# Linear attention with routed experts on one core: the state sets in a row, results a quad later, scatters in batches

## The reference

```
xn = layernorm(x)                            # x: 8 x 1024 x 128, float32
q, k, v = xn @ W_qkv, 16 heads of 8; k = layernorm(k) within each head
S = 0; for each chunk of 64 tokens:
    y = S q + causal(q k^T) v;  S = S + v^T k
attn = y @ W_o
e    = argmax(xn @ centroids.T)              # one of 8 experts a token, 8192 tokens
xh   = layernorm(xn) * ln_g[e] + ln_b[e]
h    = relu(w1[e] @ xh + b1[e])              # 512 wide
ffn  = xn + sigmoid(xn . centroid[e]) * (w2[e] @ h + b2[e])
out  = x + attn + ffn
```

## Time and profile before

| what | value |
|---|---|
| device time, 3 runs | 392.41 us median, 391.08 to 395.75 |
| profiled execution: its span | 363.3 us |
| between that span and the median | 29.1 us |
| mean granted clock of TensorE | 0.986 |

### The profile page before, as it was taken

The page is one execution under the profiler, slowest core; times in us unless marked ns, Lnnn a source line. Parts: engine busy times, 40 slices in busy tenths (PEclk is TensorE's granted clock), DMA queues, the critical chain, the costliest instruction groups (busy, mean ns, idle before and its releaser), DMA issues.

```text
span 363.3 us, 17565 instructions
## 1 busy us (share of the span) xinstructions
PE 342.1 (94%) x6868; PEld 293.0 (81%) x6868; DVE 287.1 (79%) x799; ACT 241.8 (67%) x657; POOL 251.7 (69%) x245
## 2 busy tenths in 40 slices
PE   6799999998999999999999989999999999999991
PEld 6466786776787687777867879999999999999990
DVE  8888897898886888878877786788777788777860
ACT  4788687677587666757566735766666667666660
POOL 3488477789788765556455513888888888888884
PEclk9989999999999999999999999999999999999996
DMA  6220433636314021545553445555545555555420
GB/s 196 70 60 8 118 91 97 184 104 194 106 47 120 19 87 54 157 109 163 150 152 93 131 105 134 72 73 72 72 65 74 71 63 74 74 76 59 38 23 0
DMA packets 55153, 33.18 MB, mean 91 GB/s; under 512 B 5352, under 2 KB 52768, under 8 KB 55072
## 3 DMA queue, kind: packets, MB, share of 16 engines
q1 hardware_dynamic: 42800, 23.53, 23.9%
q0 software_dynamic: 12272, 8.54, 17.2%
HBM read 18.72 MB, written 13.78 MB: 89 GB/s over the span
## 4 chain that ended last, share of the span: by engine, by line
issue 25%; POOL 13%; PE 11%; DVE 1%; DMA 1%; POOLq 1%; ACT 1%; SPq 0%; DVEq 0%; ACTq 0%
POOL out_dram L494 13%; PE bank L1328 2%; PE sc L1274 2%; PE bank L1337 2%; PE bank L1222 1%; DMA out_dram<-res 1%; POOLq L71 1%; PE bank L1200 1%; PE bank L1306 1%; DVE pr L856 1%; PE bank L1209 1%; PE bank L1295 1%; PE bank L1255 1%; PE bank L1215 0%; PE bank L1233 0%
## 5 line engine op out<-in xcount | busy, mean ns | idle before, releaser
L494 POOL DMA_INDIRECT out_dram<-qx,rows x71 | 112.9, 1590 | 35.1 <-issue 22.1
L694 ACT ACTIVATE qx<-sc,b1T 128x128 f32<-128x128 f32 x280 | 79.8, 368 | 39.6 <-PE sc L1421 39.6
L420 POOL DMA_INDIRECT slots_d<-rows,pos_i x64 | 64.2, 1003 | 43.1 <-issue 11.0
L856 DVE TENSOR_TENSOR pr<-sc,causal 128x1536 f32<-128x1536 f32 (+2 forms) x33 | 63.6, 1929 | 17.4 <-PE sc L1274 17.2
L1429 PE MATMUL bank<-tokens,qx 128*128 128x128 f32 x568 | 75.3, 276 | 0.8 <-ACT qx L694 0.7
L1421 PE MATMUL sc<-wide,tokens 128*128 128x128 f32 x560 | 74.0, 275 | 0.2 <-issue 0.2
L1429 PEld LDWEIGHTS bank<-tokens,qx 128*128 128x128 f32 x568 | 69.0, 192 | 1.4 <-ACT qx L694 1.4
L1421 PEld LDWEIGHTS sc<-wide,tokens 128*128 128x128 f32 x560 | 68.1, 192 | 0.3 <-issue 0.3
L1015 DVE COPY tokens<-xT 128x1024 f32 x71 | 55.2, 778 | 0.0
L1274 PEld LDWEIGHTS sc<-qx,kT 32*64 32x64 f32 x2048 | 32.5, 132 | 16.4 <-issue 15.8
L1030 DVE SCALAR_TENSOR_TENSOR qx<-bank,rows,qx 128x128 f32<-128x128 f32 x71 | 24.9, 350 | 26.3 <-PE bank L1429 25.8
(11 more groups left out here) (167 smaller groups left out, 532.2 us busy)
## 6 DMA issues: line engine op xcount, KB each, us to landing
rows<-slots_d SPq DMA_DIRECT2D x71, 66.0 KB, 2.0
res<-in_L_attn_x_dram SPq DMA_DIRECT2D x16, 256.0 KB, 4.1
out_dram<-res SPq DMA_DIRECT2D x16, 256.0 KB, 3.4
tokens<-in_L_attn_x_dram SPq DMA_DIRECT2D x7, 512.0 KB, 4.2
w1raw<-in_L_ffn_w_dram SPq DMA_DIRECT2D x8, 256.0 KB, 4.0
w2raw<-in_L_ffn_w_dram SPq DMA_DIRECT2D x8, 256.0 KB, 4.3
out_dram<-qx,rows POOLq DMA_INDIRECT x71, 3.4
slots_d<-rows,pos_i POOLq DMA_INDIRECT x64
```

Source lines behind the costliest of these rows:

```text
L420: pool.indirect_dma_start(slots_d, bass.IndirectOffsetOnAxis(ap=pos_i[:, t:t + 1], axis=0), rows[:, t, :], None, bounds_check=E * RT * P - ...
L494: pool.indirect_dma_start(out_rows, bass.IndirectOffsetOnAxis(ap=xs[:, a, D + 2:D + 3].bitcast(U32), axis=0), ye[:, a, :], None, bounds_ch ...
L694: last = nc.scalar.activation(ht[:, k % 2, c * P:(c + 1) * P], inner(k)[:, c * P:(c + 1) * P], ACT.Relu, bias=b1T[:, bass.ds(e * FC + c, 1)])
L856: nc.vector.tensor_tensor(pr[:, h % 2, a:G, w].rearrange("p g (j t) -> p g j t", t=CH), sc[:, a * BANK:G * BANK].rearrange("p (g w) -> p g ...
```

## The change

Four parts, in all engines' orders. (1) TensorE does `products(2n-1)`, then `state_step(n)`, `inter_second(n-1)` and `inter_first(n)` behind each other; the middle state's share is added a quad later, so `y_copy` and the output of quad n - 1 wait for it. The first state difference moves from the Y bank to FB (quad 0 apart), the affinities' back transposes and the ranks to FB and into the next quad's first half, and the second transpose of a quad's end from FB to a Y bank. (2) At a quad's end the order of ScalarE is: transposes, `values_across`, `ln_root` for the quad after; VectorE has `ln_inverse` and `ln_shift` ahead of the first mask. (3) ln_g and ln_b are applied in `se_xT` as scale and bias, w1 is copied unscaled, and the fold, `b1T`, `lbb` and its load go. (4) GpSimd sends three rows behind the quad's first mask in quads 3 to 8 (two more in 7 and 8), and from quad 9 four and three a quad.

```diff
@@ tensor: the quad loop
-                scores(h)
-                if h % 2 == 0:
-                    if more:
-                        kT_project(n + 1)
-                    state_step(n)
-                    if h:
-                        products(h - 1)
-                    inter_first(n)
-                    if more:
-                        k_transpose(n + 1)
-                    if n and out_early(n):
-                        output(n - 1)
-                    if more:
-                        q_project(n + 1)
-                else:
-                    products(h - 1)
...
+                scores(2 * n)
+                if n:
+                    products(2 * n - 1)
+                    state_step(n)
+                    inter_second(n - 1)
+                    inter_first(n)
+                if n in (2, 4, 6, 8):
+                    affinities_back(n // 2 - 1)
+                if n in (3, 5, 7, 9):
+                    rank_tokens(n // 2 - 1)
+                if more:
+                    kT_project(n + 1)
+                if n == 0:
+                    state_step(0)
+                if more:
+                    q_project(n + 1)
+                    k_transpose(n + 1)
+                if n and early:
+                    output(n - 1)
...
+                scores(2 * n + 1)
+                products(2 * n)
+                if n < 8 and n % 2 == 1:
+                    affinities(n // 2)
+                if more:
+                    v_project(n + 1, FB)
...
@@ tensor: kT_project
-                    second_left(n - 2)
+
+                    pe.wait_ge(s("dsta_sb"), n)
+                if n in (3, 5, 7, 9):
+                    pe.wait_ge(s("aff_sb"), n // 2)
+                if n in (4, 6, 8, 10):
+                    pe.wait_ge(s("rank_sb"), n // 2 - 1)
@@ gpsimd
+            for n in range(LATE):
+                norm = n + 1 < NCH
+                mask_scores(2 * n)
+                if n >= 3:
+                    send_rows(3 if norm else 3)
+                if norm:
+                    ln_norm(n + 2, range(4))
+                    ln_norm(n + 2, (4,))
+                mask_scores(2 * n + 1)
+                state_middle(n)
+                if not norm:
+                    send_rows(2)
+                state_end(n)
+                if n + 1 < LATE:
+                    values_own(n + 1)
@@ scalar: expert stage
-                nc.scalar.activation(xsT[:, k % 2, :], SC[k % 2][:, 0:P], ACT.Copy).then_inc(s("sex_sb"), 1)
...
+                of = SC[k % 2][:, 0:P] if k > 1 else FB[:, k * P:(k + 1) * P]
+                nc.scalar.activation(xsT[:, k % 2, :], of, ACT.Identity, scale=gT[:, bass.ds(e, 1)],
+                                     bias=lbT[:, bass.ds(e, 1)]).then_inc(s("sex_sb"), 1)
@@ vector
-            def b1_fold(e):
...
+                if norm:
+                    ln_inverse(n + 2)
+                    ln_shift(n + 2)
+                if n == 0:
+                    dstate_first(n)
+                score_mask(2 * n)
+                if n:
+                    dstate_first(n)
```

397 lines of the change are left out of this document (164 added, 233 removed).

## The result

The changed kernel takes 435.02 us (median of 4 runs, 433.27 to 436.62) against 391.75 us (4 runs, 389.93 to 395.75) for the kernel before: a ratio of 1.1085, 95% interval 1.1009 to 1.1161. The forecast was 393.4 with a range up to 399. It is wrong by 42 us.

The account below looks back on a forecast made before the run. TensorE's own instructions were taken to set the quads' pace except in 3 and 5. Terms +1.7 +3.2 +1.4 -1.2 -4.0 -0.1 = +1.0 took the span from 363.3 to 364.3; with 29.1 carried, 393.4 us, range 386.5 to 399.

Parts of the forecast that it names:

- The base of the sum: Whole kernel: the 29.1 us between the profiled span of 363.3 and the median of 392.4 was carried unchanged.
- Scatters in the late quads, seven of 1.28 in 11.7, fit: GpSimd in late quads: seven scatters of 1.28 us fit in a quad of 11.7, costed at nothing.
- Quads 10 to 14: Late quads: each takes 11.75 us instead of 12.54, 4.0 us gained in all, bounds nothing to 6.
- K + 7.6: Late quads: the next quad starts 7.6 us after the k projection's start K, at 11.7 from the quad's start.
- the waits hide the small stalls on issue: Late quads, TensorE: small issue stalls, one of 0.32 us, are hidden by waits, so a quad is taken at 11.75.
- The gain from fewer changes of tile shape: TensorE, each quad: 7 changes of tile shape instead of 11 at 0.15 us, up to 0.6 us of 12.5.
- Early even quads: Quads 2, 4 and 6: norm steps and state difference delay the k projection, 13.4 us each, +3.2 in all.
- Quads 3 and 0: Quad 3: GpSimd's three sends delay its normalised rows, 15.6 us, +1.4; quad 0: VectorE's norm steps go first, +1.7.
- Quads 1, 5, 7, 8, 9: These quads end 0.2, 0.25, 0.4, 0.0 and 0.4 us earlier, -1.2 in all, bounds -3 and +2.
- Fold, scale and bias: Fold leaving VectorE, scale and bias in ScalarE's expert-row copy: +0.07 us a slot, bounds 0 and 0.2, hidden, costed at nothing.
- The rivals: Three alternatives: TensorE bound everywhere, 383.4 or 388, chance 0.25; GpSimd bound, 398.1, 0.25; drains saved needlessly, 397.4, 0.05.
- GpSimd becomes the bound of quads 3 to 6: Rival: GpSimd's 13.1 us a quad grows to 14 or more, +5.7 in all, 398.1 us; chance 0.25.

Follow-up runs that it names:

- b1_before: The kernel before, unchanged, profiled a second time: 388.49 us, span 386.7.
- e1_spread: The changed kernel with its scatters one at a time again as before the change, each behind its own signal: 417.94 us, 1.0675 of before.
- e5_light: The changed kernel with scatters in threes, released behind the state sets and the first products, ahead of TensorE's long instructions: 419.44 us, 1.0717 of before.
- e2_batched: The kernel before with only its scatters batched as the change does it: 430.20 us, 1.1008 of before.
- e3_held: The changed kernel with all 64 scatters held back until behind the last quad: 475.39 us.
- e7_plain: The changed kernel with plain DMAs of the same bytes in the batches' places and the true scatters behind the last quad: 472.09 us.
- m2_late_norm: e3_held with VectorE's two norm steps moved back behind the mask and the first state difference: 466.07 us.
- e9_before_held: The kernel before with its 64 scatters held back behind the last quad: 448.75 us.
- n1_fold: The kernel before with only VectorE's fold and its load removed and scale and bias applied in ScalarE's copy: 389.26 us, 1.0008 of before.
- e6_landed: The changed kernel with single scatters as in e1_spread, each from quad 9 also waiting until the one before has landed: 470.62 us.

## Why the prediction was wrong, step by step

**The base of the sum.** "The page gives no time of its own beside the span, so I carry the 29.1 us between it and the median of 392.4 unchanged." This is the step that failed first. Around the span lie 1.8 us (b1_before: 388.49 less 386.7). The spans of b1_before and of the earlier trace rows are 23.4 us apart, time in which the scatters starved TensorE, in the timed executions and not in the profiled one; the other 3.9 are what the median of 392.4 is above b1_before's 388.5. A cost of the scatters was so carried over as a constant, though the change moves the scatters. All that I read from the earlier trace rows for quads 3 to 14 was of an execution that is not like those timed. It also hid the one resource that the change loads harder. 29.1 us is 7% of the time and should have been a question.

**"Scatters in the late quads, seven of 1.28 in 11.7, fit", at nothing.** They fit on GpSimd. They cost TensorE 236.7 - 208.2 = 28.5 us over the quads in the kernel before, single (b1_before), and 283.7 - 233.6 = 50.1 in the changed one, batched: +21.6. With the order's 25.4 (233.6 - 208.2) that makes 47.0, and the spans are 433.8 - 386.7 = 47.1 apart (the medians of the one round that timed both 43.3). By e1_spread's profile against that of the changed kernel, undoing the batches wins 14 of the 21.6 (269.5 against 283.7 at the last scores); but that execution is the slowest of its four, and by the medians it is 17. By e5_light a part of this may be the place and not the batching.

The two sums don't simply add, either. In the kernel before the batches cost more than in the changed one: e2_batched has its last scores at 278.3, so 278.3 - 208.2 = 70.1. On top of batches the new order costs 283.7 - 278.3 = 5.4 and without any scatter 25.4. So the scatters' new places alone bring nearly the whole loss, and so far as they are there, the order adds little.

**Quads 10 to 14, "5 x 0.8 = 4.0 us gained".** Without any scatter they take 65.5 us changed and 60.8 before: +4.7 instead of -4.0. Some of them did come out at 11.7 as forecast (quads 10 in e3_held and 10 and 11 in e7_plain and m2_late_norm), so the chain that I worked out was right (k projection at 3.9 for 4.1, the next quad 7.75 behind it for K + 7.6, though the terms given for it add up to only 7.4). What I left out is the late instructions, 1.4, 1.6, 2.1 and 0.7 us of idle time in quads 11 to 14, 5.8 of the 7.0 by which the five exceed 5 x 11.7, and the clock (0.97 against 1.00). I wrote that "the waits hide the small stalls on issue". The new order took away the waits behind which, by that reading, the fetch caught up. The gain from fewer changes of tile shape, up to 0.6 us a quad by the earlier trace rows, is inside the 11.7 at most, and nothing of it reached the time. The Trainium skill ("TensorEngine Tiling (Array Packing)", Key Properties) says that a change of tiling mode drains TensorE. The traces agree: a set of 16 small records takes 0.61 us from start to start in the earlier trace rows, and 0.46 in quad 10 of e3_held, where a set of the same shape follows. It just was not what decided.

**Early even quads, 13.4 each.** Held: 13.7, 14.6 and 14.8. In quad 2 the chain came out step by step: the mask 2.30 us in (2.35 forecast), TensorE waiting 0.74 on the first difference (0.8), the k projection at 5.6 (5.45). Quads 4 and 6 hold one gap of late instructions each besides, 1.45 and 1.58. But the norm steps ahead of the mask are the smaller part of it. m2_late_norm moves them back, and quad 2 is still 13.2, where e9_before_held has 12.0. There the k projection comes at 5.0, not 5.6, and waits for VectorE's copy of the affinities instead. TensorE in quad 2, e3_held and then m2_late_norm:

```profile
46.34 0.63 PE L1125 MATMUL bank<-ident,affT 128*128 128x128 f32 x4 [0.74 <-DVE dstate L826]
47.39 1.10 PE L1147 MATMUL bank<-xT,wqkv 128*128 128x512 f32 x2 [0.43 <-issue]
```

```profile
45.22 1.10 PE L1146 MATMUL bank<-xT,wqkv 128*128 128x512 f32 x2 [0.59 <-DVE aff L862]
```

So of the 1.7 us that quad 2 loses, 0.5 is the norm steps. The rest stands with what else the order puts ahead of the k projection, the state sets and the affinities' transposes and copy; no run moved these alone.

**Quads 3 and 0.** Quad 3 was to be 15.6 because GpSimd's three sends hold up the rows that it normalises. That step failed: the quad is 17.03 with the sends and 17.0 in e3_held without any. There TensorE waits 2.2 us for the first difference ahead of the ranks, and the clock of the stretch falls to 0.90; m2_late_norm has 14.4. So VectorE's order made it, with the clock, and not GpSimd's sends. Quad 0 was to be 15.1 behind the norm steps and measured 16.1 to 16.7 (TensorE waits 4.0 us there on the second difference; the clock of the stretch is 0.80 in the changed kernel); moving the steps back wins 1.5. There the mechanism was right and the size too small.

**Quads 1, 5, 7, 8, 9.** Held: 12.7, 17.9, 14.4, 14.2 and 13.6, against forecasts of 12.6, 14.75, 12.9, 12.7 and 12.8. Quad 1 is right; the others hold one gap of late instructions each, 1.0 to 1.8 us of idle time, and quad 5 ran at a clock of 0.81.

**Fold, scale and bias.** The copy went from 294 to 477 ns, 0.18 a slot where I had 0.07 with a bound of 0.2; hidden, as said: n1_fold is 1.0008.

**The rivals.** None was this. "GpSimd becomes the bound of quads 3 to 6" looked at GpSimd's length alone (13.33 busy of 21.17 in quad 4: it was not the bound). The missing rival was that GpSimd's work slows TensorE without a semaphore between them, and the trace that I had could not show it: it has no break beside a scatter that isn't one of late instructions. Those it did show. The stall of 0.32 us on "issue" in the earlier trace rows, which I set aside as small, stands behind record 8129, 193 modulo 256, and so was a sign of the other thing that I left out.

## What to carry to other kernels

Compare the profiled execution's span with the spans or times of the timed ones before reading a row of it; here they should differ by 2 us, differed by 29, and a second profile of the same kernel would have shown why. Indirect DMAs made by GpSimd are not free for TensorE: here they cost 0.4 to 1.1 us each of its time where it runs sets of small matmuls (28.5 / 64 single, 50.1 / 64 and 70.1 / 64 batched), however idle GpSimd and the DMA queues are. Batches are the worst of it where they meet such sets; groups of three placed ahead of long matmuls cost no more than single ones (e5_light). A longer row of small matmuls can be slower than the same sets with waits between: by the places of the gaps, these waits are where TensorE's instruction supply catches up.

## What was unexpected

- A scatter that writes nothing starves TensorE as much as one that writes 66 KB: pieces of 4 or 5 records 0.75 us apart. Where scatters stand alone, in e6_landed from quad 10 on, 10 of the 13 breaks beside them end 1.31 to 1.34 us behind the scatter's start, most having begun 0.7 behind it, and the other three end at 0.56 to 0.59; GpSimd's own interval is 0.97. A plain DMA of the same bytes from the same queue does not.
- The same program ran once with a span of 363.3 and 36 times at 385.8 to 394.6, and the breaks beside scatters are what differs. What decides is not known, nor whether the changed kernel has such an execution; none of its 4 had (431.2 to 434.5).
- In the expert stage 71 scatters with addition, 1590 ns each, run beside TensorE and cost it nothing (120.00 busy of 120.00): it issues 1078 matmul records in those 120 us, 9 a us, where a scores set issues 64 in 0.95.
- TensorE's instructions come in packets of about 256, and a row of small matmuls without a wait loses 1.0 to 2.1 us of idle time, in e3_held at nine of some forty-five such boundaries, always behind the same record of the packet.
